# Bias adds, group scales and output transposes moved in a graph and feed-forward kernel

## The reference

```
h  = layernorm(x)
n  = segment_sum(h[src], dst) / max(degree, 1)
g  = h @ W_self + n @ W_neigh + b
g  = where(g >= 0, g, 0.01 * g)
x1 = x + g / max(norm(g), 1e-12)              # norm over the 512 features
y  = layernorm(x1)
for each weight w of gate, up, down, in groups of 128 inputs:
    s  = mean(abs(w)) + 1e-5                  # one scale for each row and group
    wq = clip(round(w / s), -1, 1) * s
out = x1 + (silu(y @ gate_q.T) * (y @ up_q.T)) @ down_q.T
```

## Time and profile before

| | |
|---|---|
| median of 3 runs | 371.93 us (371.62 to 371.94) |
| the profiled execution: device time | 372.08 us |
| its span in the trace | 370.1 us |
| TensorE busy | 340.7 us (92%) |
| VectorE busy | 312.9 us (85%) |
| ScalarE busy | 235.4 us (64%) |
| GpSimd busy | 173.8 us (47%) |

### The profile page before, as it was taken

How to read it: one execution, slowest core, us unless ns; L and a number is a source line. 1 busy time by engine, 2 the same in 40 slices (tenths; PEclk the granted TensorE clock), 3 DMA queues, 4 the chain that set the end, 5 groups by cost and what they waited for, 6 DMA issues and landing times.

```text
span 370.1 us, 5903 instructions
## 1 busy us (share of the span) xinstructions
PE 340.7 (92%) x1741; PEld 260.3 (70%) x1741; DVE 312.9 (85%) x746; ACT 235.4 (64%) x637; POOL 173.8 (47%) x218
## 2 busy tenths in 40 slices
PE   2988999999999999999866999999999999999992
PEld 1444555555555667778655888889899898889981
DVE  2599999898898517999688799999999988999994
ACT  2174877777768224775556777777676678776660
POOL 3003343342122210111003456788788887799990
PEclk9999999999999999999989999999999999999997
DMA  7951222322212101200000000000000000000214
GB/s 229 291 143 45 71 83 60 86 58 70 74 50 81 31 1 30 75 25 0 3 0 2 0 1 2 0 3 1 0 3 0 2 2 2 0 0 3 90 34 156
DMA packets 9412, 16.70 MB, mean 45 GB/s; under 512 B 1062, under 2 KB 1886, under 8 KB 9378
## 3 DMA queue, kind: packets, MB, share of 16 engines
q1 hardware_dynamic: 9300, 16.21, 15.4%
q10 hardware_dynamic: 78, 0.08, 0.1%
HBM read 13.73 MB, written 2.56 MB: 44 GB/s over the span
## 4 chain that ended last, share of the span: by engine, by line
PE 63%; DVE 23%; ACT 7%; POOL 3%; issue 2%; POOLq 0%; DVEq 0%; ACTq 0%
PE bank L1198 39%; PE bank L1087 9%; PE bank L1127 5%; DVE hot_dst L904 4%; DVE tq_gu L841 3%; PE bank L1048 3%; DVE tq_d L841 2%; ACT mag_early L642 2%; PE bank L464 2%; DVE bn L946 2%; DVE x_sb L943 1%; DVE bn L827 1%; PE bank L1039 1%; DVE z L925 1%; DVE hot_src L900 1%
## 5 line engine op out<-in xcount | busy, mean ns | idle before, releaser
L1198 PE MATMUL bank<-x_hi,t_gu 128*128 128x378 f32 (+1 forms) x264 | 96.2, 364 | 3.6 <-DVE x_lo L960 2.8
L1198 PE MATMUL bank<-x_lo,t_gu 128*128 128x378 f32 (+1 forms) x264 | 94.7, 359 | 0.0
L1087 PE MATMUL bank<-w_sb,xnT 128*125 128x512 f32 x160 | 87.6, 635 | 2.2 <-ACT z L672 1.5
L997 DVE SCALAR_TENSOR_TENSOR g_acc<-bank,nscale,g_acc 128x378 f32<-128x378 f32 (+1 forms) x99 | 64.3, 650 | 11.9 <-PE bank L1198 11.3
L561 POOL TENSOR_SCALAR thr<-absum 128x4 f32<-128x4 f32 (+1 forms) x34 | 15.8, 464 | 112.2 <-ACT mag_early L642 79.5
L997 DVE SCALAR_TENSOR_TENSOR u_acc<-bank,nscale,u_acc 128x378 f32<-128x378 f32 (+1 forms) x99 | 64.1, 647 | 0.6 <-PE bank L1198 0.6
L595 POOL TENSOR_TENSOR hh<-sg,u_acc 128x378 f32<-128x378 f32 (+1 forms) x32 | 35.1, 1097 | 57.6 <-ACT sg L770 57.4
L1048 PEld LDWEIGHTS bank<-hot_dst,hot_src 128*125 128x125 bf16 x281 | 32.2, 137 | 39.9 <-issue 22.2
L585 POOL TENSOR_TENSOR acc<-acc,d_one 128x378 f32<-128x378 f32 (+1 forms) x57 | 60.1, 1055 | 0.0
L1198 PEld LDWEIGHTS bank<-x_hi,t_gu 128*128 128x128 f32 x264 | 50.4, 191 | 8.1 <-DVE x_lo L960 3.5
L1198 PEld LDWEIGHTS bank<-x_lo,t_gu 128*128 128x128 f32 x264 | 50.6, 192 | 3.6
(11 more groups left out here) (107 smaller groups left out, 549.4 us busy)
## 6 DMA issues: line engine op xcount, KB each, us to landing
raw<-in_L_ffn_w_gate SPq DMA_DIRECT2D x11, 256.0 KB, 2.7
raw<-in_L_ffn_w_up SPq DMA_DIRECT2D x11, 256.0 KB, 2.6
out_x<-x_sb SPq DMA_DIRECT2D x10, 224.0 KB
raw<-in_L_ffn_w_down SPq DMA_DIRECT2D x8, 256.0 KB, 2.6
x_sb<-in_x SPq DMA_DIRECT2D x1, 1344.0 KB
w_sb<-in_L_gnn_W_neigh SPq DMA_DIRECT2D x1, 1024.0 KB, 6.2
w_sb<-in_L_gnn_W_self SPq DMA_DIRECT2D x1, 1024.0 KB, 7.1
raw<-in_L_ffn_w_down SPq DMA_DIRECT2D x4, 192.0 KB, 2.3
```

Of the source, the lines that this page charges most:

```text
L997: nc.vector.scalar_tensor_tensor(out=to, in0=bank_of(u, what)[:, 0:w], scalar=nscale[:, j:j + 1], in1=to, op0=ALU.mult, op1=ALU.add).then_ ...
L1087: last = nc.tensor.matmul(to[0:TP, :], xnT[:, t, k * TP:(k + 1) * TP], w_sb[:, k, half * D:(half + 1) * D], start=k == 0, stop=k == KD - 1)
L1198: last = nc.tensor.matmul(to, w, parts[h], start=h == 0, stop=h == 1)
```

## The change

Three things. First, GpSimd computes only `thr` for each load; `nscale` of all 132 groups comes in one operation behind the last load, with a semaphore of its own, `nscales`, which the first take on ScalarE and the first on VectorE wait for. VectorE's ternary waits for `thr` alone. Second, GpSimd's ten bias adds no longer stand among the slots of the first stage: they come behind its last `thr` and behind the last copy of `a_t` (`block_out` = NB), ahead of the scales of the second stage's loads. Third, `by_act` gives D3 of unit 31 (NU - 2) to ScalarE and GpSimd as well as D1, and the O pieces of tiles 0 to 2 go from the end of turn 33 (behind D of unit 30) to the end of turn 34 (behind D of unit 31); those of tiles 0 and 1 are added by GpSimd as before. The orders of all engines follow from `pieces`.

```diff
@@ by_act
-            return what in ("G0", "U0") or what in ("D1", "D3")[:max(0, min(2, NU - 1 - u))]
+            return what in ("G0", "U0") or what in ("D1", "D3")[:2 if u < NU - 1 else 0]
@@ pieces
-                if n == (u + LAG + 1 if u < NU - 3 else NU + LAG - 1):
+                if n == {FINAL[0]: FINAL[0] + LAG + 1, FINAL[1]: NU + LAG - 2, FINAL[2]: NU + LAG - 1}[u]:
@@ GpSimd
                 nc.gpsimd.tensor_scalar(thr[:, js], absum[:, js], 0.5 / P, 0.5 * Q_EPS, ALU.mult, ALU.add).then_inc(scales, 1)
-                nc.gpsimd.tensor_scalar(nscale[:, js], absum[:, js], 1.0 / P, Q_EPS, ALU.mult, ALU.add).then_inc(scales, 1)
-
-            for slot in range(SLOTS + 8):
-                t, i = divmod(slot, 8)
-                for j in jobs_in(slot, 7):
-                    l, g = job_load[j]
-                    if g == loads[l][1] - 1:
-                        scales_of(l)
-                if i == 4 and 1 <= t <= NT:
-                    if t == 1:
-                        pool.wait_ge(bias_in, 16)
-                    pool.wait_ge(z_out, t)
-                    nc.gpsimd.tensor_tensor(z[:, t - 1, :], z[:, t - 1, :], bias_b[0:TP, :], ALU.add).then_inc(z_done, 1)
+
+            for l in range(LOADS1):
+                scales_of(l)
+            pool.wait_ge(bias_in, 16)
+            pool.wait_ge(block_out, NB)
+            for t in range(NT):
+                pool.wait_ge(z_out, t + 1)
+                nc.gpsimd.tensor_tensor(z[:, t, :], z[:, t, :], bias_b[0:TP, :], ALU.add).then_inc(z_done, 1)
             for l in range(LOADS1, len(loads)):
                 scales_of(l)
+
+            nc.gpsimd.tensor_scalar(nscale[:], absum[:], 1.0 / P, Q_EPS, ALU.mult, ALU.add).then_inc(nscales, 1)
@@ ScalarE, take (VectorE's take the same with dve)
+                if took[u, what] == 1:
+                    act.wait_ge(nscales, 1)
                 act.wait_ge(piece_ready, index[u, what] + 1)
@@ VectorE, ternary_of
-                dve.wait_ge(scales, 2 * job_load[j][0] + 2)
+                dve.wait_ge(scales, job_load[j][0] + 1)
```

More of the change, by code:

```diff
@@ L207, in gnn_ffn @@
         scales = sem("scales")
+        nscales = sem("nscales")
         ternary = sem("ternary")
@@ L984, in take @@
                 to = {"G": g_acc[:, u % 2, 0:w], "U": u_acc[:, u % 2, 0:w], "D": acc[:, k, nodes_of(u)]}[what[0]]
+                if took[u, what] == 1:
+                    dve.wait_ge(nscales, 1)
                 dve.wait_ge(piece_ready, index[u, what] + 1)
```

## The result

| | before | after |
|---|---|---|
| median, lowest and highest of 20 runs | 371.94 us (371.35 to 373.87) | 369.88 us (368.21 to 372.57) |
| the profiled execution: device time | 372.08 us | 368.42 us |
| its span in the trace | 370.1 us | 366.4 us |
| VectorE busy | 312.9 us (85%) | 307.5 us (84%) |
| GpSimd busy | 173.8 us (47%) | 162.0 us (44%) |

The ratio of after to before is 0.994 [0.992 to 0.996]: 2.1 us faster. The forecast was 368.7 us in a range of 367.4 to 371.6, so the sign and the range held. The profiled execution of after, at 368.42, is one of the quick ones of its kernel, and that it agrees with the forecast is partly luck, as the table shows.

A forecast was written before the change was run, and what follows sets the result against it. Most of the chain was taken to be TensorE, with VectorE's own work behind it in the second stage. 1.4 + 0 + 1.8 = 3.2 us off the profiled 372.08 gave 368.88, with the median 0.15 lower 368.7; range 367.4 to 371.6.

The forecast's parts named there:

- First stage: To 127.7 us: four TensorE stalls for ScalarE's z copy cost 2.2 us, of which the edits win 1.4.
- near 63.5: First-stage z stall of 0.44 us, behind two adds and two nscale waits: all of it goes.
- 87.81: First-stage z stall of 0.65 us: 0.5 goes, as VectorE then meets the limit of five hot_dst buffers.
- 112.00: First-stage z stall of 0.35 us: nothing gained, as VectorE had been waiting for TensorE before it.
- 41.71: First-stage z stall of 0.77 us: 0.45 goes, as nscale waits alone make ScalarE late.
- Rival 2: First stage: ScalarE's own order makes its copy late, TensorE's stalls stay, nothing gained: 370.1 us; chance 0.12.
- Second stage: Ten bias adds there cost 0, bounds 0 to +0.5; leak(0) may wait one add, 1.27 us, inside 3.8 slack.
- Rival 1: Second stage: ten back to back GpSimd adds starve VectorE, leak(0) 7.6 to 8.6 us late: 373.0 us; full form 0.11.
- End: Last turns: VectorE's 0.98 idle, D3's 0.53 and small gaps go, 1.8 us less, bounds 1.0 to 2.1.
- Outputs: At the end: six tiles in one run at 338 GB/s, up to 0.5 us later, taken as 0; last issue not held.
- rival 3: End bound by outputs: six tiles in one run and SP's queue order leave 1.0 of 1.8: 369.5 us; chance 0.07.
- rival 1's weak form: Second stage: leak(0) waits for four or five adds, costing 1 to 2.5 us: 369.7 to 371.2 us; chance 0.06.

The follow-up runs named there:

- bias_alone: Kernel before with only the bias adds moved behind the first stage, nscale still for each load: 370.82 us, ratio 0.9968.
- nscale_alone: Kernel before with only the single nscale operation, bias adds and output transposes as before: 370.72 us, ratio 0.996.
- three_edits_more: Changed kernel with twelve early unread matmuls, D3 of unit 31 on VectorE, ScalarE's z copy one slot earlier, eleven unread matmuls before feed-forward: 364.54 us, 0.9797.
- whole_again: The changed kernel once more, with no further edit: 369.34 us, ratio 0.9926 to before.
- tail_alone: Kernel before with only the end edit: second group's transposes behind unit 31's down products, its D3 by ScalarE and GpSimd: 370.28 us, 0.9951.

## Why the prediction was right, and where it wasn't

**First stage: forecast -1.4, measured -1.23.** The size is right, two of its terms are not. Named stall by stall: near 63.5 all gone (counted 0.44, right); 87.81 gone wholly (counted 0.5 of 0.65); 112.00 unchanged (right); 41.71 unchanged, where I counted 0.45 of 0.77. That step read a VectorE lag of 0.28 us ahead of the copy as its cause. bias_alone and nscale_alone both leave it at 0.6, and in three_edits_more the one edit at this place, ScalarE's copy a slot earlier, removes it. The sum came near partly by luck: 0.45 too much at this stall, and 0.29 too little at the two in the middle. Rival 2 was right for this stall and the last in so far as the relief of VectorE left them, wrong for the two between. The edits are not additive: each takes most of the same two stalls.

**Second stage: forecast 0, measured 0.** Rival 1, the one on the slower side, is dead: VectorE waited for one add each time, with ten queued behind each other. leak(0) lost 1.17 us of the 1.27 allowed, inside 3.8 of slack. The rule of the Trainium skill (SBUF — State Buffer, "Who interferes with whom"), that the lock holds for one whole instruction, had spoken against this rival, and the trace agrees, with 1.86 us for leak(0) against 12.99 for the adds. The reverse case is not explained by it: `thr`, 0.19 us when free, still took 1.71 us in after (at 32.55) between VectorE operations, as it took 1.70 in the earlier trace rows. So I had drawn from one engine's loss to the other's, and that is where rival 1 was overpriced. The ten adds ran from 125.71 to 138.70, where I had said 126.8 to 139.5, the whole 1.1 us early by the start of this execution; their pitch was 1.30 us, and the `thr` behind them came at 138.78, in time.

**End: forecast -1.8, measured -1.98 in the computation.** The wait for D1 went, D3's 0.53 went, unit 31's matmuls went into TensorE's idle time; as the sum had it. What the computation needed was in time; SP's issues were not, as follows.

**Outputs: forecast 0, bound 0.5, measured +1.0 to +1.66.** This is the step that failed, and it failed twice. The forecast let SP issue every DMA in 0.33 us and a little more, tiles 0 to 2 in time, and concluded that the last tile isn't held. In whole_again and tail_alone one issue took 1.55 us, and the last tile's issue ended 1.7 and 1.8 us behind its add instead of 0.35; in after it was 0.56. And it computed the landing of six tiles from 338 GB/s, the best microsecond of before, so that the DMA engines could cost 0.5 at most. Over the six microseconds of the run the mean was 251 GB/s in after, and from the last issue to the end it took 0.7 us more than in before. (The mean of 199 in whole_again is no measure of the landing, since the DMA engines stood half idle for want of issues.) The mechanism was rival 3's, in which six tiles and SP's queue eat a part of the end; it gave 369.5, nearer to the median than the forecast. It acted in all four profiles with the turns moved, all six tiles written and D3 on GpSimd (gaps of 4.24 to 4.99 us), beside the forecast and not in place of it, and in none of the three with D3 on VectorE (3.24 to 3.44).

**The start: not in the forecast.** The sum went off one profiled execution, 372.08 us. Its start was 1.44 us later than after's, which no edit touches. That the profile of after came out near the forecast is luck of its early start. Hence the difference of 3.7 us between the profiles where the medians differ by 2.1. What the sum should have been: -1.23 - 1.98 + 1.0 to 1.66 = -1.55 to -2.2, or 369.7 to 370.4, and 369.88 was measured. One sum in the forecast's chances is a little off, too: the 0.83 for faster is the forecast with rivals 2 and 3, and with most of rival 1's weak form, as it says, it would be 0.87 or so.

**What stays open.** The spread of after's runs, 368.2 to 372.6, is made in part of the start (over 2 us between profiles) and the outputs (0.7 us between two profiles). An execution of 372 us of after wasn't caught in a profile. Its granted clock is on record, 0.981 to 0.990 in the three slowest runs against 0.995 in the six quickest, so TensorE spent more of them at the lower level; where, is not known. Nor is it known why before, which has the same start, hardly ever is quick: early matmuls gave before 0.9 us and after 2.4. The first stage gives 1.0 us back there, and half pace in its last transposes takes 1.02 us in two of its three profiles, but one of these two had no early matmuls, so that the account doesn't close.

## What to carry to other kernels

Cost the landing of outputs from a window as long as the run of transfers, not from its best microsecond; lay out the issues of the queue beside the times at which the data are ready, for one late issue holds all behind it; and ask for every microsecond that an end is shortened how much of the transfers it had been hiding. Ahead of a sum over one profile, cut a second profile of the same kernel at the same events: what differs there (here 0.4 to 2 us at the start and 1.0 at the end) belongs to no edit. With a wait that ends with a slower engine's copy, ask also where in that engine's order the copy stands; two of the four stalls stayed when VectorE was relieved and went when ScalarE's copy moved by one slot.

## What the runs showed of the hardware

- Ten GpSimd adds in a row do not shut VectorE out of SBUF: each VectorE operation waited for one add (1.86 and 1.58 us against 0.69). In the other direction a GpSimd operation of 0.19 us took 1.71.
- TensorE's first matmuls run at half of their later pace (0.85 us against 0.43 a pass) up to a moment that differs from execution to execution by more than 2 us; the view shows a granted clock of 1.00 there, but the trace has no clock record before that moment. Twelve unread matmuls from 3.30 us on make the full pace start with the first real one: 3.70 instead of 5.17 to 6.62 us for eight, 2.4 us of the median.
- The same twelve transposes after the same 2.90 us of idle took 1.55 to 1.76 us in three profiles and, at a granted clock of 0.50, 2.89 in two; after 1.64 or 1.65 us of idle 1.54 or 1.55 in all of five.
- Six outputs of 256 KB behind each other left at 251 GB/s in the mean of six microseconds, with 338 in the best microsecond of before.
- SP took 0.3 to 0.45 us to issue most of the output DMAs, but 1.55 us for one of them in two of the four profiles with the whole end edit, and everything behind it in the queue left later.
